# A message-passing kernel: the counts pass with four dense tiles a chunk and its rows in three bf16 parts

## The reference, cut to what matters

```python
h = jnp.maximum(_layernorm(x, axis=-1), 0.0)
x = x + _L2_gnn_ref(h, src, dst, L2_gnn_weight, L2_gnn_bias)
...
ones_e = jnp.ones(src.shape[0], dtype=features.dtype)
deg_out = jnp.clip(jax.ops.segment_sum(ones_e, src, num_segments=n), 1.0)
deg_in = jnp.clip(jax.ops.segment_sum(ones_e, dst, num_segments=n), 1.0)
h = features * jax.lax.rsqrt(deg_out)[:, None]
agg = jax.ops.segment_sum(h[src], dst, num_segments=n)
agg = agg * jax.lax.rsqrt(deg_in)[:, None]
out = agg @ weight + bias
return jax.nn.relu(out)
```

## Time and profile before

| what | value |
|---|---|
| median of 3 runs | 5463.11 us (5455.49 to 6915.47) |
| the profiled execution | 5453.59 us |
| its span, first to last instruction | 5451.4 us |
| granted TensorE clock, mean | 0.83 of 2.4 GHz |
| TensorE, GpSimd, VectorE, ACT busy | 75%, 67%, 55%, 30% |

### The profile page before, as it was taken

One profiled execution on the slowest core, in us unless ns is written; L12 is line 12 of the kernel. 1 busy time (PEld: TensorE's weight loads), 2 busy tenths in 40 slices (PEclk: granted clock), 3 DMA queues, 4 the chain that ended last, 5 costly groups with the idle time before them and its releaser, 6 DMA issues.

```text
span 5451.4 us, 88258 instructions
## 1 busy us (share of the span) xinstructions
PE 4081.7 (75%) x26225; PEld 3597.7 (66%) x26225; DVE 2992.9 (55%) x10670; ACT 1657.1 (30%) x3531; POOL 3668.0 (67%) x3340
## 2 busy tenths in 40 slices
PE   3777766676775488888887578886688888688886
PEld 2655555555664377777777466665577877588886
DVE  3655555555551677777776444445444555444445
ACT  3544444444442343333332322222211111111111
POOL 0788888888885277777773676761677777277773
PEclk7877777777777688888887799998799999799998
DMA  6666666666665222222221211110334343344442
GB/s 203 130 115 118 112 118 114 113 114 115 115 107 103 58 56 56 56 55 54 55 54 24 67 52 50 50 50 21 114 129 139 125 143 125 99 149 157 144 156 89
DMA packets 405518, 531.75 MB, mean 98 GB/s; under 512 B 136752, under 2 KB 321689, under 8 KB 398521
## 3 DMA queue, kind: packets, MB, share of 16 engines
q0 software_dynamic: 199680, 221.72, 22.4%
q1 hardware_dynamic: 205496, 305.85, 17.7%
HBM read 374.16 MB, written 153.13 MB: 97 GB/s over the span
## 4 chain that ended last, share of the span: by engine, by line
PE 40%; issue 16%; DMA 15%; DVE 14%; POOL 9%; DVEq 2%; SPq 1%; ACT 1%; POOLq 0%; ACTq 0%
DMA sums<-G,idx 14%; POOL sums L736 9%; PE psF L1210 8%; PE psC L1210 8%; PE psC L1143 4%; PE psE L1196 4%; PE psD L1196 4%; PE psA L1133 3%; DVE S L1732 3%; PE psB L1185 2%; PE psA L1185 2%; DVE early L1721 1%; DVEq L490 1%; DVE G L1638 1%; PE psD L1148 1%
## 5 line engine op out<-in xcount | busy, mean ns | idle before, releaser
L711 POOL DMA_INDIRECT G<-table,idx x1664 | 1595.5, 959 | 857.0 <-issue 496.1
L736 POOL DMA_INDIRECT sums<-G,idx x832 | 1283.7, 1543 | 370.5 <-issue 200.4
L693 POOL DMA_INDIRECT G<-table,idx x832 | 785.7, 944 | 285.1 <-issue 253.8
L967 ACT COPY arena<-psA 128x600 f32<-128x600 f32 x312 | 206.0, 660 | 1222.9 <-PE psA L1185 1159.0
L1083 PE MATMUL psE<-arena,stage 128*128 128x128 f32 x832 | 211.3, 434 | 441.5 <-ACT G L887 441.3
L1083 PEld LDWEIGHTS psE<-arena,stage 128*128 128x128 f32 x832 | 181.1, 321 | 526.1 <-ACT G L887 526.1
L1210 PE MATMUL psC<-arena,stage 128*128 128x144 f32 (+1 forms) x3822 | 504.4, 291 | 0.0
L1210 PE MATMUL psF<-arena,stage 128*128 128x144 f32 (+1 forms) x3822 | 504.1, 292 | 0.0
L1210 PEld LDWEIGHTS psF<-arena,stage 128*128 128x128 f32 x3822 | 493.1, 201 | 0.0
L1210 PEld LDWEIGHTS psC<-arena,stage 128*128 128x128 f32 x3822 | 492.1, 200 | 0.0
L1494 DVE TENSOR_TENSOR arena<-psB,G 128x1024 f32<-128x1024 f32 x104 | 127.4, 1225 | 648.7 <-PE psB L1064 648.7
(11 more groups left out here) (281 smaller groups left out, 7997.0 us busy)
## 6 DMA issues: line engine op xcount, KB each, us to landing
adjacency<-arena SPq DMA_DIRECT2D x26, 2400.0 KB
arena<-adjacency SPq DMA_DIRECT2D x26, 2400.0 KB
acc<-in_src_row SPq DMA_DIRECT2D x104, 512.0 KB
arena<-in_dst_row SPq DMA_DIRECT2D x104, 512.0 KB
G<-table,idx POOLq DMA_INDIRECT x2496
sums<-G,idx POOLq DMA_INDIRECT x832, 3.4
sums<-arena SPq DMA_DIRECT2D x4, 3300.0 KB, 26.9
table<-stage SPq DMA_DIRECT2D x28, 448.0 KB, 3.0
```

What stands on the lines that cost most here:

```text
L693: pool.indirect_dma_start(G[st.r][:, t * width:(t + 1) * width], None, tables[n], bass.IndirectOffsetOnAxis(ap=idx[st.r][:, t:t + 1], axis ...
L711: pool.indirect_dma_start(G[at.r][:, t * D:(t + 1) * D], None, tables[n], bass.IndirectOffsetOnAxis(ap=idx[at.r][:, t:t + 1], axis=0)).the ...
L736: pool.indirect_dma_start(sums_dram[t % SUMS], bass.IndirectOffsetOnAxis(ap=idx[st.r][:, t:t + 1], axis=0), G[st.r][:, t * TW:(t + 1) * TW ...
L967: A.copy(dense_at(at.g, m.loaded + j, k % GROUP), counts_in((k * m.built + j) % 2)).then_inc(mixed["kept"], 1)
```

## The change

The counts pass has four dense tiles of a chunk and four gathered ones, where it had three and five. Its planes are bf16 (`dense16`; counts are small whole numbers). The normalized rows go to another place (`h_split`) and are split into three bf16 parts whose sum is the float32 row: ACT copies a batch to bf16 (`first_part`), VectorE subtracts this, casts the rest, and subtracts again. `dense_sums` multiplies each block three times, once with each part. ACT waits for the table's writes before the pass, since its planes lie over `h_split`. The other passes keep their numbers.

```diff
--- before.py
+++ after.py
@@ -137,7 +137,7 @@
     GROUPS = CHUNKS // GROUP
     STORED = 2
     mixes = {}
-    for n, what in ((2, (3, 0, False, True)), (3, (2, 0, True, False)), (4, (3, STORED, False, False))):
+    for n, what in ((2, (4, 0, False, True)), (3, (2, 0, True, False)), (4, (3, STORED, False, False))):
         mixes[n] = Mix(n, *what, CHUNKS, mixes.get(n - 1))
     assert BLOCKS % BJ == 0 and CHUNKS % ROWS == 0 and CHUNKS % TURN == 0 and TURN % ROWS == 0
 
@@ -184,6 +184,13 @@
         big = [arena[:, behind + k * CHUNK:behind + (k + 1) * CHUNK] for k in range(5)]
         dense = [arena[:, behind + 7 * CHUNK - 3 * PLANE:], arena[:, 0:3 * PLANE]]
         assert 3 * PLANE <= behind
+        half_planes = 4 * PLANE // 2
+        dense16 = [arena[:, behind + 7 * CHUNK - half_planes:].bitcast(BF16), arena[:, 0:half_planes].bitcast(BF16)]
+        h_split = arena[:, behind + 7 * CHUNK - BLOCKS * D:]
+        h_part = [arena[:, half_planes:half_planes + BLOCKS * D // 2].bitcast(BF16),
+                  stage[:, 0:BLOCKS * D // 2].bitcast(BF16), stage[:, BLOCKS * D // 2:BLOCKS * D].bitcast(BF16)]
+        h_rest = [arena[:, k * BW:(k + 1) * BW] for k in range(2)]
+        assert half_planes + BLOCKS * D // 2 <= behind + 7 * CHUNK - BLOCKS * D
         dloc = [sb(f"dloc{k}", TILES) for k in range(2)]
         ident = sb("ident", P)
         iota = sb("iota", P)
@@ -299,7 +306,7 @@
         phases = (
             f"{norm} h tr lhs prod rows",
             f"tr turned mm abs relu exp ln lhs prod upd resid {norm} h scored kept",
-            f"counts1 deg1 root1 lhs prod upd resid {norm} rows",
+            f"counts1 deg1 root1 lhs prod upd resid {norm} rows h",
             f"counts1 deg1 root1 lhs prod upd biased resid {norm} h tr turned rows",
             "lhs prod upd biased neg prelu h tr turned rows",
             "lhs prod upd biased neg prelu resid")
@@ -495,9 +502,13 @@
             return (psA, psB)[k][:, :].rearrange("p (b s) -> p b s", b=2)[:, :, 0:KEYS // 2]\
                 .rearrange("p b (h w) -> p b h w", w=SLOTS)
 
-        def dense_at(g, t, place):
-
-            return dense[g][:, t * PLANE:(t + 1) * PLANE]\
+        def planes(m, g):
+
+            return (dense16 if m.counts else dense)[g]
+
+        def dense_at(m, g, t, place):
+
+            return planes(m, g)[:, t * PLANE:(t + 1) * PLANE]\
                 .rearrange("p (b h s) -> p b h s", b=2, s=SEG)[:, :, :, place * SLOTS:(place + 1) * SLOTS]
 
         def segments(ap, n):
@@ -547,7 +558,7 @@
                 def one(j):
                     reached(sp, nd[n]["rows"], j + 1)
                     sp.dma_start(tables[n][bass.ds(j * BW, BW), :].rearrange("(b p) f -> p b f", p=P),
-                                 tiles(stage[:, batch(j)], BJ)).then_inc(table_out, 16)
+                                 tiles((h_split if n == 2 else stage)[:, batch(j)], BJ)).then_inc(table_out, 16)
                 with sp.Fori(0, NJ) as j:
                     one(j)
 
@@ -792,7 +803,7 @@
                             batch_before(act, s["rows"], j)
                     for b in range(BJ):
                         at = bass.ds(j * BW + b * D, D)
-                        to = stage[:, at] if to_stage else h7[:, b * D:(b + 1) * D]
+                        to = h_split[:, at] if to_stage else h7[:, b * D:(b + 1) * D]
                         ins = A.activation(to, X[:, at], ACT.Relu,
                                            bias=col["bias"][:, bass.ds(j * BJ + b, 1)],
                                            scale=col["scale"][:, bass.ds(j * BJ + b, 1)])
@@ -964,7 +975,7 @@
                             act.wait_ge(adj_moved[at.g], i * 16)
                         for j in range(m.built):
                             act.wait_ge(mixed["counted"], m.made(at.c, j + 1))
-                            A.copy(dense_at(at.g, m.loaded + j, k % GROUP),
+                            A.copy(dense_at(m, at.g, m.loaded + j, k % GROUP),
                                    counts_in((k * m.built + j) % 2)).then_inc(mixed["kept"], 1)
                 return turn
 
@@ -981,7 +992,18 @@
             act.wait_ge(acc_ready, 2)
             batches(act, acc_to_lhs(2))
             sqrt_of(2)
-            batches(act, normalized(2, to_stage=True))
+            rows_of = normalized(2, to_stage=True)
+
+            def first_part(j):
+                reached(act, nd[2]["rows"], j + 1)
+                A.copy(h_part[0][:, batch(j)], h_split[:, batch(j)]).then_inc(nd[2]["h"].sem, 1)
+
+            for j in range(NJ):
+                rows_of(j)
+                if j > 0:
+                    first_part(j - 1)
+            first_part(NJ - 1)
+            act.wait_ge(table_out, 16 * (TABLE_DMAS[1] + NJ))
             mixed_act(2)
             act.wait_ge(acc_ready, 3)
             roots_of_degrees(3)
@@ -1206,10 +1228,13 @@
                             pe.wait_ge(adj_moved[at.g], at.i * 16 + (GROUPS // 2 + 1) * 16)
                         if not at.first:
                             pe.wait_ge(mixed["spread"], m.spread(at.group * GROUP - GROUP, 0))
+                    terms = h_part if m.counts else [stage]
                     for h in range(part * BLOCKS // GROUP, (part + 1) * BLOCKS // GROUP):
-                        ins = M.matmul(segments((psC, psF)[at.g][:, 0:m.dense * SEG], m.dense), stage[:, h * D:(h + 1) * D],
-                                       segments(dense[at.g][:, 0:m.dense * PLANE], m.dense)[:, :, h * SEG:(h + 1) * SEG],
-                                       start=(h == 0), stop=(h == BLOCKS - 1))
+                        for q, term in enumerate(terms):
+                            ins = M.matmul(segments((psC, psF)[at.g][:, 0:m.dense * SEG], m.dense), term[:, h * D:(h + 1) * D],
+                                           segments(planes(m, at.g)[:, 0:m.dense * PLANE], m.dense)
+                                           [:, :, h * SEG:(h + 1) * SEG],
+                                           start=(h == 0 and q == 0), stop=(h == BLOCKS - 1 and q == len(terms) - 1))
                     if part == GROUP - 1:
                         ins.then_inc(mixed["applied"], 1)
 
@@ -1691,7 +1716,11 @@
             batches(dve, node_2)
             reached(dve, s2["bn"], NJ)
             norm_columns(2, dinv[:, 0:BLOCKS])
-            reached(dve, s2["rows"], NJ)
+            for j in range(NJ):
+                reached(dve, s2["h"], j + 1)
+                link(V.tensor_tensor(h_rest[j % 2], h_split[:, batch(j)], h_part[0][:, batch(j)], ALU.subtract))
+                link(V.tensor_copy(h_part[1][:, batch(j)], h_rest[j % 2]))
+                V.tensor_tensor(h_part[2][:, batch(j)], h_rest[j % 2], h_part[1][:, batch(j)], ALU.subtract)
             reached(dve, nd[3]["counts"], 1)
             V.tensor_copy(dcount[:, :], psD[:, 0:2 * BLOCKS])
             V.tensor_copy(srclo[:, :], srcl[:, :])
```

## The result

The changed kernel takes 5507.06 us (median of 4 runs, 5500.60 to 5511.04), the kernel before 5462.05 us in the same comparison. The ratio is 1.0089, with a 95% interval of 1.0076 to 1.0102 (the two medians alone give 1.0082): slower by 0.9%, clear of its own noise and within 2%. One of the four runs of the kernel before took 6915 us and does not count in the ratio. The forecast was 5497 us.

A forecast was written before the change was run, and what follows sets the result against it. Bound: the counts pass's 6.47 us chunk, VectorE's one-hots (2.31 us) then TensorE's products. 25 + 11.5 + 2.2 = +38.7 us on the profiled 5453.6 us gives 5492, put at 5497 us allowing for the median; range 5465 to 5565 us.

The forecast's parts named there:

- ahead of the pass: Node work before the counts pass: ACT's bf16 copies and VectorE's split delay everything behind by 11.5 us (8.5 to 13).
- the chunks: Counts pass, 104 chunks: each 0.24 us longer, 25 us in all (5 to 60).
- the tail: End of the counts pass: the last group's serial additions, 16 for 12 at 0.55 us each, +2.2 us.
- Dense products: TensorE, counts pass: 3822 bf16 pairs at 82.5 ns, 315 us for 312, +3 us, if weight loads stay hidden.
- Rival A: Dense products: weight loads come out from under the matmuls, 122.5 ns a pair, +153 us, 5650 us; chance 12%.
- One gathered tile less: Each chunk: 0.24 us less on TensorE, one one-hot (0.20 us) less on VectorE, GpSimd from 6.25 to 5.0 us.
- One dense tile more: Each chunk: VectorE's fourth pair (0.45) and addition (0.20), less one one-hot (0.20), start gathered products 0.45 us later.
- A chunk: Counts pass: 0.45 - 0.24 + 0.03 = +0.24 us a chunk, between +0.05 and +0.58.
- rival B: Counts pass: clock falls more often, 1.6 us a stretch, up to +83 us, 5580 us; 6%, milder form 5%.
- C: Counts pass: VectorE's added work is off the path, -0.21 to -0.41 us a chunk, 5434 to 5455 us; chance 5%.
- D: Counts pass: GpSimd's 6.25 us sets part of the pace, a gather less returns 10 us, 5487; within the forecast's 77%.
- Fewer gathers therefore buy nothing by themselves: Counts pass: no row shows TensorE waiting for gathered rows, though GpSimd's 6.25 us a chunk is close to 6.47.

The follow-up runs named there:

- e1: Changed kernel with three dense tiles and five gathered ones, bf16 planes and three terms kept: 5404.4 us, ratio 0.9912 to the kernel before.
- e6: Changed kernel with plain copies of as many table rows for the counts pass's gathers (wrong rows added): 5471.5 us, ratio 1.0027 to the kernel before.
- e5: Kernel before, with the changed kernel's split into three parts made ahead of the counts pass and read by nobody: 5462.2 us, ratio 1.0006.
- e3: Kernel before, TensorE's counts pass reordered: half the dense products after two counts, half after the last, gathered products last: 5395.1 us, ratio 0.9896.
- e4: Changed kernel with the same new TensorE order as e3: 5274.5 us, ratio 0.9673 to the kernel before.
- e10: e3 with plain copies in place of the counts pass's gathers (wrong rows added): 5261.9 us, single run.
- e9: Changed kernel with e4's TensorE order and the accumulator cleared ahead of the split: 5273.6 us, ratio 0.9672 to the kernel before.
- e7: Changed kernel with the accumulator cleared early, ahead of VectorE's split: 5499.0 us, ratio 1.0069 to the kernel before.
- e2: Changed kernel with a chunk's additions moved behind the float32 one-hots on VectorE: 5440.0 us, ratio 0.9980 to the kernel before.
- e8: Changed kernel with the edits of e4, e2 and e7 together: 5312.0 us, ratio 0.9727 to the kernel before.
- e11: e4 with plain copies in place of the counts pass's gathers (wrong rows added): 5279.7 us, single run.

## Why the prediction was right, point by point

The time came in the range and 10 us over the forecast, and the mechanism of the steady chunk (VectorE's work ahead of the float32 one-hots outweighs the gathered tile saved) is what the runs show. That the number is so close is partly luck, since two terms of the sum were wrong in opposite directions:

| term | forecast, us | measured, us |
|---|---|---|
| ahead of the pass | 11.5 | 0.1, taken at the ninth chunk |
| the chunks | 25 (of 104) | 41.3 (ninth to last) |
| the tail | 2.2 | 2.1 |
| behind the pass | 0 | 3.9, cause unknown |
| sum | 38.7 | 47.4 |

- *Dense products*, forecast 3 us over the pass at 82.5 ns a pair: 82 to 83 ns measured, 2.97 us a chunk for 2.94. Rival A is excluded. So is the estimate of 25 ns more a pair from the Trainium skill's figure for real streams ("TensorE: Matmul & The Clock Gate", "Back-to-back issue gap", 81 ns at 128 columns), which the traces contradict: 82 to 83 ns at 192 columns, and 62.5 ns at 144 columns in e1. Rival A's price was also read too high: its 122 ns for a float32 record with 128 columns is the whole stretch of 1.22 us by ten, and within the stretch the records stand 111 to 112 ns apart, for 122 to 123 with 144 columns.
- *One gathered tile less*, forecast -0.24 us a chunk on TensorE: -0.23 by the medians.
- *One dense tile more*: the mechanism was right, the term too small. Forecast was +0.45 us to the start of the gathered products, measured +0.51 by the medians and +0.58 in the chunk shown. The addition was 0.16 us and not 0.20; the fourth pair was 0.56 and not 0.45, and the four one-hots 0.96 us where four fifths of 1.08 are 0.86. e6 shows the cause of both: with no gather in work on GpSimd the term is 2.71 us, 0.18 less. I had priced VectorE's instructions by rows in which a gather happened to lie elsewhere.
- *A chunk*: forecast +0.24 us, measured +0.43 in the mean from the ninth chunk on. Chunks at full clock are 0.35 us longer, 33 us in all; at a group's start it is 0.41, where I had not looked. The other 8 us are rival B in a mild form: 12 stretches of 3.4 us at half clock for 6, and a chunk that holds one takes 8.36 us for 6.82 (before, 8.21 for 6.51).
- *Ahead of the pass*: the delay of 11.5 us was right (11.1), and it was wrong to put it into the sum. The fourth chunk is 5.3 us later, the sixth and the ninth 0.1. I had not asked what else is late there: before, the second to the fifth chunk wait for gathered rows, and GpSimd starts only 4.7 us later, not 11. e5 separates a part of this: with the same delay and five gathers 4.6 us are left at the ninth chunk. The changed kernel fetches four tiles a chunk and waits for none of them. The clock helps it too: before, it is at half until 3061.4 us, apart from two gaps, and in the changed kernel only until 3045.6; how much of the remaining 4.6 us each of the two gives was not separated.
- *The tail*, forecast +2.2: 24.7 us from the last gathered products to the last addition for 22.6, +2.1.
- *Rivals C and D*: C is refuted by the 2.89 us. D had its place wrong in the middle of the pass (no chunk there waited for GpSimd), but its mechanism is what holds the second to the fifth chunk of the kernel before, which the prediction had not read, and its number was right: 6.25 us was the floor close under TensorE's 6.47. "Fewer gathers therefore buy nothing by themselves" held for the middle of the pass in the order as it is, and e3, e4 and e10 show what it conceals: in an order that hides VectorE's work, the change is worth 1.26 us a chunk.

## What to carry to other kernels

Ask for each engine what the shortest possible period of a repeated stage is, and then what the order adds to it. A change that lowers the floor of one engine (here GpSimd's, 6.25 to 5.0 us a chunk) shows next to nothing while the order between two others stands above it (here 2.3 us from the first count to the gathered products, in which TensorE has 0.8 us of work), and may even lengthen that stretch; with the wait removed the same change was worth 2.2% (0.9673 for 0.9896). So try the change together with an order that hides the wait before it is dropped: of the kernels run here the changed one with TensorE's new order (e4, with e9 level) is the fastest that computes the reference, 3.3% under the kernel before. And a delay ahead of a stage is paid only as far as its slowest supplier is late as well, here 4.6 of 11 us in e5, and not even so far where that supplier has been given less to do. To see it, compare the two timelines at several points of the stage and not only at its start and its end.

## What the runs showed of the hardware that was not expected

- bf16 weight loads of 128 columns vanished wholly under bf16 matmuls of 192 columns (82 to 83 ns) and of 144 (36 of them in 2.25 us, 62.5 ns a pair). The 20 ns between the two are 48 columns, 0.42 ns each: 1 column a cycle at 2.4 GHz, and about 2.5 ns on top.
- Float32 records (a load and a matmul) stood 122 to 123 ns apart with 144 columns and 111 to 112 ns with 128, and just as far with 2 columns (L1143 of the kernel before).
- A gather in work on GpSimd lengthened VectorE's one-hots in 16 bits, but only in a part of it. Between 3150 and 3650 us of the changed kernel, 62 of the 277 low one-hots of L1747 began 0.45 to 0.75 us after the start of a gather (0.94 us long) and took 422 ns on average, up to 483. The 38 that lay wholly inside a gather but began at another time took 249 ns, as did the 119 beside no gather. The kernel before shows the same, with 341 ns for 27 such one-hots and 249 for 71 inside. No run shows what happens in that part of a gather.
- The granted clock fell to 1.2 GHz for 3.4 us 12 times between 3063 us and the last chunk of the changed kernel, 6 times in that of before and in e5, 12 in e7, 9 in e1, 3 in e6, and never there in e2, e3, e4, e8, e9, e10 and e11. It is not the longest wait of TensorE that tells them apart: in the median chunk this was 0.69 us before, 0.65 in the changed kernel and 1.16 in e3.
